# A 64-byte table dropped, so that the operand tiles of three stages begin at multiples of 512 bytes

## What is computed

```python
def L0_ffn(x, router_w, router_b, w1, b1, w2, b2):        # 8 experts, top 2, capacity 320
    gates = softmax(x_flat @ router_w + router_b)
    ...                                                    # buf[e]: the tokens of expert e
    h = gelu(einsum('ecd,edh->ech', buf, w1) + b1[:, None, :], approximate=False)
    out = einsum('ech,ehd->ecd', h, w2) + b2[:, None, :]
    return einsum('ned,ne->nd', gathered, weights)

def L1_cond(context_c, time_cond, ...):                    # 4 experts, top 2 per row, and a shared one
    for e in range(E):
        h = gelu(context_c @ ew1[e] + eb1[e], approximate=True)
        out = out + w_be[:, e][:, None, None] * mask[e][None, :, None] * (h @ ew2[e] + eb2[e])
    return out + gelu(context_c @ sw1 + sb1, approximate=True) @ sw2 + sb2

def L1_ffn(x, Wr, br, W1, b1, W2, b2):                     # 8 experts, all of them on every token
    gates = entmax_bisect(xt @ Wr + br)
    h = relu(einsum('td,edf->etf', xt, W1) + b1[:, None, :])
    return einsum('etd,te->td', einsum('etf,efd->etd', h, W2) + b2[:, None, :], gates)
```

## The kernel before

| tile | bytes | first byte | past a multiple of 512 |
|---|---|---|---|
| weights w1, w2 of e0, c1, m1 | 8 x 8192 | 69120 | 0 |
| `e0_x_hi` | 2560 | 135232 | 64 |
| `e0_h_hi`, `e0_h_lo` | 10240 each | 140352, 150592 | 64 |
| `c1_x_0hi` to `c1_x_1lo` | 4096 each | 136256 | 64 |
| `c1_h_hi`, `c1_h_lo` | 16384 each | 156736, 173120 | 64 |
| `m1_x_hi`, `m1_x_lo` | 16384 each | 136256, 152640 | 64 |
| `m1_h_hi`, `m1_h_lo` | 16384 each | 169024, 185408 | 64 |
| `e3` weights, x, h | | 69120, 134656, 142848 | 0 |

## Time and profile before

### The profile page before, as it was taken

One profiled execution on the slowest core, in us unless ns is written; L12 is line 12 of the kernel. 1 busy time (PEld: TensorE's weight loads), 2 busy tenths in 40 slices (PEclk: granted clock), 3 DMA queues, 4 the chain that ended last, 5 costly groups with the idle time before them and its releaser, 6 DMA issues. The chain is left out here.

```text
span 2338.2 us, 33811 instructions
## 1 busy us (share of the span) xinstructions
PE 2038.3 (87%) x13199; PEld 1632.2 (70%) x13199; DVE 1338.2 (57%) x2448; ACT 978.0 (42%) x1939; POOL 376.5 (16%) x308
## 2 busy tenths in 40 slices
PE   5688799999899999999999996479976767698698
PEld 3488788888687888888888785369963555366465
DVE  2765556787675446455464312656547457365796
ACT  2243446556444445445445322134433336455332
POOL 1366401233100000000000002138740000000000
PEclk8798899999999999999999998589987866899899
DMA  2654212322115021112000001355554002010000
GB/s 82 221 152 123 53 37 73 108 98 84 37 37 117 24 54 30 50 53 51 30 19 22 15 26 41 103 164 135 135 126 102 2 2 55 18 55 3 0 10 27
DMA packets 111160, 150.45 MB, mean 64 GB/s; under 512 B 6856, under 2 KB 93431, under 8 KB 110616
## 3 DMA queue, kind: packets, MB, share of 16 engines
q1 hardware_dynamic: 99836, 130.14, 18.7%
q0 software_dynamic: 11168, 18.18, 3.9%
HBM read 124.08 MB, written 24.22 MB: 63 GB/s over the span
## 5 line engine op out<-in xcount | busy, mean ns | idle before, releaser
L1810 DVE TENSOR_TENSOR m_h_lo<-m_hf,m_h_hi 128x512 fp32r<-128x512 f32 x256 | 173.7, 690 | 317.4 <-ACT m_hf L1785 313.3
L1782 ACT ACTIVATE m_h_hi<-m_h_ps,m_bT 128x512 fp32r<-128x512 f32 x256 | 176.5, 689 | 372.8 <-PE m_h_ps L396 350.2
L642 POOL DMA_INDIRECT token_sums<-e_y,slot_row x56 | 173.8, 3104 | 107.4 <-DVE e_y L768 94.0
L1785 ACT ACTIVATE m_hf<-m_h_ps,m_bT 128x512 f32<-128x512 f32 x256 | 175.0, 684 | 0.0
L727 ACT ACTIVATE e_h_hi<-e_h_ps,e_b1T 128x320 fp32r<-128x320 f32 (+1 forms) x128 | 78.0, 610 | 167.4 <-PE e_h_ps L396 162.2
L1463 DVE TENSOR_TENSOR c_h_lo<-c_hf,c_h_hi 128x512 fp32r<-128x512 f32 x120 | 92.0, 774 | 91.5 <-ACT c_hf L1413 90.6
L791 DVE TENSOR_TENSOR e_h_lo<-e_hf,e_h_hi 128x320 fp32r<-128x320 f32 (+1 forms) x128 | 72.3, 582 | 119.6 <-ACT e_hf L730 119.6
L1269 POOL TENSOR_TENSOR cT<-cT,c_yg 128x128 f32 x88 | 76.8, 872 | 271.5 <-DVE c_yg L1481 257.8
L1410 ACT ACTIVATE c_h_hi<-c_h_ps,c_b 128x512 fp32r<-128x512 f32 x88 | 60.8, 691 | 108.1 <-PE c_h_ps L396 107.4
L396 PE MATMUL m_y_ps<-m_h_hi,l_w_1hi 128*128 128x512 f32 x256 | 101.6, 397 | 3.5 <-issue 3.5
L396 PE MATMUL m_y_ps<-m_h_hi,l_w_0hi 128*128 128x512 f32 x256 | 100.6, 393 | 1.4 <-ACT m_gT L1796 1.4
(11 more groups left out here) (698 smaller groups left out, 5467.0 us busy)
## 6 DMA issues: line engine op xcount, KB each, us to landing
cT<-in_L_ffn_W_dram SPq DMA_DIRECT2D x30, 1024.0 KB, 5.3
res<-in_L_cond_ew_dram SPq DMA_DIRECT2D x22, 1024.0 KB, 5.2
cT<-in_L_ffn_w_dram SPq DMA_DIRECT2D x16, 1024.0 KB, 5.8
res<-gates_rows SPq DMA_DIRECT2D x8, 1024.0 KB, 15.5
token_rows<-d_tok SPq DMA_DIRECT2D x2, 2112.0 KB, 10.5
token_sums<-res SPq DMA_DIRECT2D x2, 2048.0 KB, 7.5
res<-token_sums SPq DMA_DIRECT2D x8, 512.0 KB, 5.6
cT<-modulation_rows SPq DMA_DIRECT2D x8, 512.0 KB, 5.9
```

The costliest lines, as they stand in the source:

```text
L642: pool.indirect_dma_start(out=sums, out_offset=bass.IndirectOffsetOnAxis(ap=st.slot_row[0:r, e, j:j + 1], axis=0), in_=y[0:r, e % 2, j, :] ...
L1782: act.activation(hs[0][:, f, :], h_ps[:, f % HB, :], ACT.Relu, bias=bT[:, at:at + 1])
L1785: act.activation(hf[:, f % HB, :], h_ps[:, f % HB, :], ACT.Relu, bias=bT[:, at:at + 1]).then_inc(act_done, 1)
L1810: dve.tensor_tensor(hs[1][:, f, :], hf[:, f % HB, :], hs[0][:, f, :].bitcast(F32), ALU.subtract).then_inc(h_ready, 1)
```

## The change

The tile `warm` is no longer allocated. The Gelu of `prepare` writes its one element into the first column of e0's bias table `b1T` instead, which the caller passes along; e0's last use of that table is the instruction before on the same engine. `FirstModulations.prepare`, which e3 calls, takes the same argument and does nothing with it.

```diff
@@ -731,7 +731,7 @@
                 if e + 1 < E8:
                     rows_hi(e + 1)
-            following.prepare(act, st)
+            following.prepare(act, st, b1T[:, 0:1])
@@ -1149,14 +1149,14 @@
-        self.act_cond, self.warm = sb("act_cond", [P, KC, B]), sb("warm", [P, 16])
+        self.act_cond = sb("act_cond", [P, KC, B])
...
-    def prepare(self, act, st):
+    def prepare(self, act, st, spare):
         act.activation(self.act_cond[:, :, :], st.condT[:, :, :], ACT.Silu)
-        act.activation(self.warm[:, 0:1], st.ones[:, 0:1], ACT.Gelu_apprx_tanh)
+        act.activation(spare, st.ones[:, 0:1], ACT.Gelu_apprx_tanh)
```

## The result

| | before | after |
|---|---|---|
| median | 2342.02 us (2340.02 to 2344.38) | 2316.12 us (2315.16 to 2319.63) |
| runs | 4 | 4 |
| the profiled execution, its own time | 2339.97 us | 2319.63 us |
| its span | 2338.2 us | 2317.9 us |

The ratio is 0.9886, with a 95% interval from 0.9872 to 0.9901.

The account below looks back on a forecast made before the run. TensorE was taken to bound the two stages after e0, and e0 except for two waits for gathers. The terms -9.9 + 2.8 = -7.1 us took the median from 2342.28 to 2335.2 us, range 2331 to 2342.5 us.

Parts of the forecast that it names:

- Step 1: The two stages after e0: 4512 matmuls of 512 columns go from 229.0 to 226.8 ns each, together -9.9 us.
- Step 2: e0's down product: matmuls go from 113.5 to 119.9 ns, 0.46 us per expert, 3.7 us for eight.
- Step 3: e0's two waits for gathers hide two of eight slower down products; six count, +2.8 us.
- step 5: Other engines: ScalarE's 689 ns activation, the moved Gelu and GpSimd's gathers were all taken as unchanged, worth nothing.
- Step 4: e0's up product, 384 matmuls: no change expected from 146.6 ns a step.
- The rule by which nothing should happen: All TensorE matmuls: distance depends on columns alone, so placement changes nothing; 2342.3 us, chance 0.16.
- The rival with +6.4 ns for the down products of c1 and m1: The two stages after e0: 2256 down matmuls slow by 6.4 ns each, +14.4 us; 2354.5 us, chance 0.07.

Follow-up runs that it names:

- e0: Not a run but a stage of the kernel, with eight experts, gathers and scatters; it takes 154.6 us before the change and 138.3 us after.
- after_split_earlier: The changed kernel with VectorE's weight split in e0 begun one loop step earlier; 2316.08 us, ratio 0.9878 to the kernel before.
- before_split_later: The kernel before, no address changed, with VectorE's weight split in e0 begun one step later for all experts but the last; 2323.28 us, ratio 0.9908.

## Why the prediction was wrong

**Step 1, c1 and m1: right.** 226.7 ns against 226.8 forecast. The stages gave 3.1 + 6.3 = 9.4 us where 9.9 were forecast, and alone they gained 10.6 us.

**Step 2, e0's down product: right in kind, the term a little large.** From 186.26 to 189.80 us the kernel after makes 30 steps, 118.0 ns each, where I had 119.9:

```profile
186.26 0.28 PE L685 MATMUL e_y_ps<-l_w_0hi,e_h_lo 128*128 128x256 f32 x1
...
189.80 0.28 PE L685 MATMUL e_y_ps<-l_w_0hi,e_h_lo 128*128 128x256 f32 x1
```

The median durations are 280 ns, between the 276 and 283 of the earlier trace rows. Over all of e0 a step from one 128-slot piece to the next takes 118.4 ns in the mean, before 114.2, and one between 64-slot pieces 115.8, before 114.7. So the long pieces lose some 4 ns and the short ones some 1, where I gave both 6.4. The loss is 138.3 - 135.1 = 3.2 us for all eight experts, in the two kernels without a wait, of which these steps account for about 2.0; 3.7 was my upper end.

**Step 3, the cover of the wait: this step failed, with the last sentence of step 5.** I took the two waits as fixed, hid two down products behind them and said that the gathers "are counted in the wait of step 3, and I take them as unchanged". The earlier trace rows held an 8.14 us gather, and I read it as the length of GpSimd's own work, and so with the 8.85 us scatter at the head of that chain. (The 27 us that I gave the chain run to TensorE's release at 217.41; GpSimd's own end is at 215.03, after 24.8 us, and the two long operations are 17 of these.) I didn't ask why this gather takes nine times as long as others of the same size. Had I put VectorE's rows beside it, I would have seen it begin 0.06 us after the start of an unbroken series and end 0.78 us after that series' end, and that the +0.46 us per expert of step 2 (0.25 in the traces) moves these two against each other. The two waits and what follows them were worth 19.5 us, and they hung on where the gather begins: 0.06 us behind the start of the series it was held, 0.41 us ahead of it it was not, and no run has a place between. So e0 gave 19.5 - 3.2 = 16.3 us, where I had a loss of 2.8.

**Step 4, e0's up product: right.** 45 steps in 6.60 us are 146.7 ns, against 146.6:

```profile
177.83 0.31 PE L396 MATMUL e_h_ps<-e_x_hi,l_w_0lo 128*128 128x320 f32 x1
...
184.43 0.32 PE L396 MATMUL e_h_ps<-e_x_hi,l_w_0lo 128*128 128x320 f32 x1
```

**Step 5, ScalarE: right.** `m_h_hi` takes 690 ns, and it waits for TensorE for 346.9 us, before 350.2.

**The rivals.** None of them had the waits gone, though the prediction's last sentence said that a wait of 6.6 us more or less is as much as the whole forecast. That was a rival with a price, and it should have had a chance and a place in the range: both waits gone would have given 2335.2 - 13.2 = 2322 us even without the clock (2323 with the two down products that they hid). The rule by which nothing should happen is refuted by m1's 226.7 ns. The rival with +6.4 ns for the down products of c1 and m1 is refuted too.

## What to carry to other kernels

When a queue's operation is several times as long as its sisters, ask what holds it, and read the other engines at its first and last moment; how far apart the two starts are gives a first idea of how small a change elsewhere can remove or bring the wait. Here a slowdown of 0.25 us per expert on TensorE removed 19.5 us, and moving VectorE's block by one step did the same on purpose (gain 19.7 us) with no address changed. Start addresses of stationary and moving tiles are worth a few ns per matmul in either direction, and the best place differs with the number of columns, so read the distance from start to start in each stage, and test a place in each before aligning all. Where two engines depend on one another, moving the work of one moves the other too (`after_split_earlier`), so read both starts again after the change.

## What the runs showed of the hardware

- TensorE's distance per matmul depends on where the stationary tile begins relative to the moving one: 226.7 to 234.2 ns with 512 columns, 113.4 to 120.0 with 256. The place that is best for 256 columns (64) is among the worst for 512.
- A gather or scatter that GpSimd issues can be held through an unbroken series of VectorE instructions with SBUF inputs, for 6.9 to 11 us in the rows above. It then does nearly all its work: a gather ends 0.78 to 0.86 us after the series, a scatter 1.42 to 1.50 us, whether VectorE goes idle or not.
- What decides who gets in is only in part known. A gather 0.40 us ahead of the series took 0.90 us where it was done before the cast and 2.13 where it wasn't. In the series of 11 instructions that has no pause, every gather and scatter that began 0.06 to 2.8 us after its start was held to its end. Shorter series can let one in: at the start of e0 a gather begins at 99.15 us in the kernel before, lasts 4.38 us and ends 2.28 us before its series of 6 does. In `before_split_later` none is held. There VectorE is idle for 0.18 us two instructions ahead of the cast. The scatter under way begins 0.08 us after the first of the subtractions, as the one of 8.85 us in the earlier trace rows does, and takes 2.89; the cast takes 1.43 us in place of 1.21. The next scatter begins at 165.86 us amid the rest of the series and lasts 2.59 us, although nothing pauses there. So the pause goes with getting in, but it doesn't explain the second scatter, and no run here tells more.

```profile
162.58 0.87 DVE L791 TENSOR_TENSOR e_h_lo<-e_hf,e_h_hi 128x320 fp32r<-128x320 f32 x2
163.63 0.49 DVE L791 TENSOR_TENSOR e_h_lo<-e_hf,e_h_hi 128x320 fp32r<-128x320 f32 x1 [0.18 <-ACT e_hf L730]
164.04 1.43 DVE L740 CAST l_w_0hi<-cT 128x2048 fp32r<-128x2048 f32 x1
```
```profile
156.81 0.90 POOL L628 DMA_INDIRECT e_taken<-token_rows,slot_row  x1 [0.30 <-issue]
162.66 2.89 POOL L642 DMA_INDIRECT token_sums<-e_y,slot_row  x1 [4.94 <-DVE e_y L768]
165.86 2.59 POOL L642 DMA_INDIRECT token_sums<-e_y,slot_row  x1 [0.31 <-issue]
```
